# Attention, expert tiles and last norms of a Mamba and mixture-of-experts layer in one block, with rows routed in two parts

## The reference

```python
x = layernorm(x + mamba2(x) + x)
# one feed-forward layer:
qkv = x @ w_qkv                     # 16 heads of 8, causal attention in each row
o = attention(q, k, v) @ w_o
h = layernorm(x + o, g1, b1)
probs = softmax(h @ wg)             # 8 experts, top 2, weights made to sum to 1
h1 = gelu(h @ w1[e] + bb1[e])       # 128 -> 512, tanh form
y = h1 @ w2[e] + bb2[e]             # 512 -> 128
f = layernorm(h + sum of w * y, g2, b2)
x = layernorm(x + f)
```

## Time and profile before

| | |
|---|---|
| three runs | 1036.42, 1039.88 (median), 1048.26 us |
| the profiled execution | 1042.99 us, of which the span of the trace is 1041.2 us |
| TensorE busy | 749.1 us (72%) |
| VectorE busy | 649.8 us (62%) |
| ScalarE busy | 504.0 us (48%) |
| GpSimd busy | 393.9 us (38%) |
| DMA | 72.34 MB, 69 GB/s over the span |

### The profile page before, as it was taken

The page is one execution under the profiler, slowest core; times in us unless marked ns, Lnnn a source line. Parts: engine busy times, 40 slices in busy tenths (PEclk is TensorE's granted clock), DMA queues, the critical chain, the costliest instruction groups (busy, mean ns, idle before and its releaser), DMA issues. The chain is left out here.

```text
span 1041.2 us, 18849 instructions
## 1 busy us (share of the span) xinstructions
PE 749.1 (72%) x5297; PEld 505.1 (49%) x5298; DVE 649.8 (62%) x1639; ACT 504.0 (48%) x987; POOL 393.9 (38%) x500
## 2 busy tenths in 40 slices
PE   5788887887482669989898988888710999997000
PEld 3565666555352334535353544443310999997000
DVE  3888888896265747858586869772150454554585
ACT  3566555542171036545455555565400666675144
POOL 1233332233210012353535354644543355554254
PEclk8989988888595569989899999996855899999555
DMA  1000000000185312342424242312011222220241
GB/s 43 16 21 26 26 6 25 26 16 11 58 280 159 116 49 65 94 110 71 113 75 117 71 115 82 87 49 68 21 41 53 73 84 81 73 83 29 83 121 41
DMA packets 87082, 72.34 MB, mean 69 GB/s; under 512 B 10931, under 2 KB 78138, under 8 KB 87006
## 3 DMA queue, kind: packets, MB, share of 16 engines
q1 hardware_dynamic: 81726, 60.29, 20.7%
q0 software_dynamic: 5280, 11.13, 3.3%
HBM read 44.05 MB, written 22.12 MB: 64 GB/s over the span
## 5 line engine op out<-in xcount | busy, mean ns | idle before, releaser
L1350 ACT ACTIVATE pb<-psB 128x512 f32<-128x512 f32 (+1 forms) x352 | 186.2, 558 | 187.5 <-PE psB L1629 182.7
L1414 DVE TENSOR_REDUCE mx<-psB 128x1 f32<-128x384 f32 (+3 forms) x352 | 208.2, 633 | 92.8 <-PE psB L1611 92.5
L1609 PE MATMUL psB<-kx,qx 72*128 72x384 bf16 (+3 forms) x512 | 145.7, 336 | 19.2 <-DMA kx<-k_parts 19.1
L1629 PE MATMUL psB<-qx,kx 75*128 75x256 bf16 (+3 forms) x512 | 132.4, 320 | 29.5 <-DMA qx<-mparts 24.2
L1310 POOL TENSOR_SCALAR_AFFINE_SELECT pb<-pb 128x512 f32<-128x512 f32 x128 | 81.1, 639 | 162.7 <-ACT pb L1350 162.0
L1644 PE MATMUL psB<-pb,vx 128*32 128x512 f32 (+3 forms) x1024 | 104.3, 481 | 13.7 <-POOL pb L1310 13.7
L1611 PE MATMUL psB<-hide,ident 128*128 128x128 bf16 x512 | 109.7, 239 | 0.0
L1880 POOL DMA_INDIRECT results<-y_e,dest x72 | 70.0, 972 | 78.8 <-DVE y_e L1947 71.9
L1629 PEld LDWEIGHTS psB<-qx,kx 75*128 75x128 bf16 x512 | 44.9, 102 | 110.0 <-ACT pb L1350 52.7
L1940 DVE TENSOR_TENSOR pre<-psE,biases 128x512 f32<-128x512 f32 x72 | 49.8, 691 | 56.2 <-PE psE L1978 49.9
L1986 PE MATMUL psE<-w2s,gT 128*128 x576 | 80.0, 282 | 4.3 <-ACT gT L1909 4.3
(11 more groups left out here) (246 smaller groups left out, 1334.1 us busy)
## 6 DMA issues: line engine op xcount, KB each, us to landing
qx<-q_parts SPq DMA_DIRECT2D x96, 96.0 KB
kx<-k_parts SPq DMA_DIRECT2D x96, 96.0 KB
hin<-slots SPq DMA_DIRECT2D x72, 64.5 KB
ys<-results SPq DMA_DIRECT2D x16, 256.0 KB, 3.1
q_parts<-qpart SPq DMA_DIRECT2D x8, 384.0 KB
k_parts<-kpart SPq DMA_DIRECT2D x8, 384.0 KB
xin<-in_L_attn_X SPq DMA_DIRECT2D x8, 256.0 KB
x_rows<-x1o SPq DMA_DIRECT2D x8, 256.0 KB
```

Source lines behind the costliest of these rows:

```text
L1350: nc.scalar.activation(pb[step % PBUF][:, h0:h0 + heads, 0:width], src, ACT.Exp).then_inc(exp_ready, 2 if u == NEXP - 1 else 1)
L1414: nc.vector.tensor_reduce(mx[:, h0:h0 + heads, qt], ps[:, S_BANK + u % banks, 0:heads * width].rearrange("p (h n) -> p h n", n=width), AX. ...
L1609: nc.tensor.matmul(out, qx[q][0:QK_ROWS, h0 + j, qt * P:(qt + 1) * P], kx[q][0:QK_ROWS, h0 + j, 0:width], start=True, stop=False)
L1629: ins = nc.tensor.matmul(ps[:, E_BANK + u % E_BANKS, j * width:(j + 1) * width], kx[q][0:MAX_ROWS, 4 * g + h0 + j, kt * P:(kt + 1) * P], q ...
```

## The change

`attention_layer`, `experts` and `last_norms` become one function with one block and no barrier in it. Rows 0 to 4 and rows 5 to 7 are routed apart: each part has regions of its own in `slots`, its own counts, plan (26 steps) and fills. Part 0 needs at most 2 x 4 x 5 + 7 = 47 tiles, part 1 at most 31, together 78 (`JOBS`) in place of 72. The plan of part 0 and its fills stand in row 6's list.

Tiles go in "beats". In beat n TensorE does down(n), up(n+2), turn(n+3); ScalarE the turned copy of n+2, gelu(n+1) and `gate_result(n-1)`, which multiplies the result by the token's gate; VectorE the bias add of n+1 and the result of n; GpSimd stores tile n-2; SyncE loads tile n+7 and the w1 of tile n+5. Beats -3 to 6 stand in row 7's list, at slots 4, 8, ... 40. Behind row 7 comes a new list, `after()`, with beats 7 and up, and beside them what ends row 7, the routing of row 7, plan and fills of part 1, and the last norms: of rows 0 to 4 one each four beats from beat 52 on, of rows 5 to 7 in beats 83 to 85, behind the last tile.

w1 is no longer kept: each tile's w1 (256 KB) is loaded from DRAM into one of four buffers, at an offset of its own. The copy of w1 on ScalarE goes, as does the cast of the destination on VectorE: the payload carries it as an integer and also the gate. w2 loads in rows 1 and 2, all biases in row 3 (those of the first layer in pieces of 4 bytes). x1 is loaded again for each row's last norm. The last norms' two weighted sums (eight 128x128 operations per row) become two 128x512 additions. The tile buffers lie over the first row pair's q and k, the norms' over the second's.

The diff, cut to its core:

```diff
+SPLIT = 5
+PART_ROWS = (SPLIT, BATCH - SPLIT)
+PART_TILES = [TOPK * TILES * rows + E - 1 for rows in PART_ROWS]
+FIRST_TILE = [0, PART_TILES[0]]
+JOBS = sum(PART_TILES)
+RING = 12
...
+PLAN_ROW = SPLIT + 1
+PLAN_AT = [4 + i // 2 for i in range(PLAN)]
+FILL_AT = [8 + 3 * e for e in range(E)]
+FIRST_BEAT = -3
+EARLY_BEATS = {4 + 4 * i: FIRST_BEAT + i for i in range(10)}
+AFTER_BEAT = FIRST_BEAT + len(EARLY_BEATS)
+EARLY_TILES = AFTER_BEAT + 3
+TAIL = {"last heads": 1, "last out": 2, "last norm": 3, "last normalise": 5, "last gain": 5, "turn h": 8, "logits": 9,
+        "gate": 15, "ranks": 15}
+TAIL_CHAIN = [10 + i // 3 for i in range(14)] + [16 + i // 3 for i in range(CHAIN - 14)]
+TAIL_SCATTER = [19 + i for i in range(TOPK * TILES)]
+TAIL_PLAN = [19 + i // 3 for i in range(PLAN)]
+TAIL_FILL = [27 + e // 2 for e in range(E)]
+NORM_AT = [FIRST_TILE[1] + 5 + 4 * b for b in range(SPLIT)] + [JOBS + 5 + i for i in range(BATCH - SPLIT)]
+NORM_STEPS = {"sum": 0, "rstd 1": 0, "shift 1": 1, "norm 1": 1, "gain 2": 2, "residual": 3, "rstd 2": 3, "shift 2": 4, "norm 2": 4,
+              "store": 6}
...
+            def load_tile(j):
+                for g in range(2):
+                    if j == FIRST_TILE[g]:
+                        sp.wait_ge(planned[g], PLAN)
...
+                        sp.wait_ge(filled[g], 16 * E)
+                        sp.wait_ge(dead_filled, 32)
+                at = offset(sp, 0, j, SLOTS - P)
+                wait(sp, stored[j % RING], j // RING * 16)
+                sp.dma_start(hin[j % RING][:, :], slots[bass.ds(at, P), :]).then_inc(h_loaded[j % RING], 16)
+
+            def load_w1(j):
+                at = offset(sp, 3, j, (E - 1) * P)
+                wait(sp, up_ps, j - 3)
+                sp.dma_start(w1t[j % 4][:, :], w1.rearrange("e d f -> (e d) f")[bass.ds(at, P), :]).then_inc(w1_loaded[j % 4], 16)
...
+            def load_norm(b):
+                q = b % 2
+                if b in (0, SPLIT):
+                    tiles = FIRST_TILE[1] if b == 0 else JOBS
+                    for k in range(RING):
+                        sp.wait_ge(stored[k], 16 * ((tiles - k + RING - 1) // RING))
...
+                wait(sp, sum_ready, b - 1)
+                for k in range(TOPK):
+                    sp.dma_start(ys[q][:, k, :, :], results.rearrange("(k b t p) d -> k b p t d", k=TOPK, b=BATCH, p=P)[k, b]).then_inc(moe_in[q], 16)
+                wait(sp, lr_ready, b - 1)
+                sp.dma_start(x1r[q][:, :, :], x1_rows[b]).then_inc(x1_in[q], 16)
...
+            def store_result(j):
+
+                wait_apart(pool, gated, j + 1, pool_passed)
...
+            def turned(j):
+                act.wait_ge(ehT_ps, j + 1)
+                wait(act, up_ps, j - 1)
+                nc.scalar.activation(hTe[j % 2][:, :], ps[:, ht_bank(j), 0:P], ACT.Copy).then_inc(ehT_sb, 1)
+
+            def gelu(j):
+                act.wait_ge(pre_ready, j + 1)
+                wait(act, y_ps, j - 1)
+                nc.scalar.activation(gT[j % 2][:, :, :], pre[j % 2][:, :, :], ACT.Gelu_apprx_tanh).then_inc(g_ready, 1)
+
+            def gate_result(j):
+                act.wait_ge(y_ready, j + 1)
+                nc.scalar.activation(y[j % RING][:, :], y[j % RING][:, :], ACT.Copy, scale=hin[j % RING][:, D + 1:D + 2]).then_inc(gated, 1)
...
+                    elif what == "beat":
+                        if 0 <= n + 2 < JOBS:
+                            turned(n + 2)
+                        if 0 <= n + 1 < JOBS:
+                            gelu(n + 1)
+                        if 0 <= n - 1 < JOBS:
+                            gate_result(n - 1)
...
+            def moe_sum(b):
+                q = b % 2
+                dve.wait_ge(moe_in[q], (b // 2 + 1) * (16 * TOPK))
+                nc.vector.tensor_tensor(s0[q][:, :, :], ys[q][:, 0, :, :], ys[q][:, 1, :, :], ALU.add).then_inc(half_sum, 1)
+                dve.wait_ge(half_sum, b + 1)
+                wait(dve, n1_ready, b - 1)
+                nc.vector.tensor_tensor(s1[q][:, :, :], s0[q][:, :, :], h_all[:, b * TILES:(b + 1) * TILES, :], ALU.add).then_inc(sum_ready, 1)
...
+                    if what == "beat":
+                        if 0 <= n < JOBS:
+                            down(n)
+                        if 0 <= n + 2 < JOBS:
+                            up(n + 2)
+                        if 0 <= n + 3 < JOBS:
+                            turn(n + 3)
```

910 lines of the change are left out of this document (378 added, 532 removed).

## The result

The changed kernel takes 1061.16 us (median of 4 runs, 1059.63 to 1072.07), the kernel before beside it 1038.15 us (4 runs, 1026.85 to 1048.26). The ratio is 1.028, with a 95% interval of 1.016 to 1.040: slower, by more than the 1 per cent that the forecast took for no change. The forecast was 1013 us, with a range to 1046.

What follows compares the result with a forecast made beforehand. The prediction took a sum of stages, each with its own limit, to bound the kernel. 778 to row 7's last exponentials + 201 beats + 35 end = 1014 span, giving a 1013 us median; eight in ten between 980 and 1046.

Steps and rivals of the forecast that it cites:

- What bounds the kernel, the serial stages: Whole kernel: the end is set by a sum of stages, with 147 us of serial stages that the change overlaps.
- Rows 0 to 6 ... Sum +7; bounds 0 and +15: Attention rows before row 7: plan 4 us, masks delayed by fills 1, w2 and bias loads 2; together 7 us longer.
- Row 7, 70 us: Last attention row: 44 us plus 26 for eight gelu beats with table loads on ScalarE; exponentials end at 778.
- Beats, 201 us: Beats 7 to 77, behind row 7: 81 + 3 + 34 + 83 us, with SyncE at 2.4 us per beat, VectorE beside the norms.
- tiles 1.9 apart: Sign that the forecast is wrong: tiles come every 1.9 us, so SyncE's work is hidden.
- The first 31 beats: Row 7's last steps, routing, scatter and fills of part 1: 31 x 2.4 + 7 = 81 us, +3 for tile 47's wait.
- The next 14: Beats between the first 31 and the norms: 14 x 2.4 = 34 us at SyncE's pace.
- Beside the norms: Last 26 beats, five norms: VectorE decides, 13.7 us per norm and 4 beats, 83 us in all.
- The end, 35 us: Behind the last tile: path to the last loads, three norms at VectorE's pace 21 us, 3.2 to the end; 35 in all.
- TensorE's clock falls, and it is slower: Rival, chance 0.12: waiting in longer beats lowers TensorE's clock to 1.2 GHz, a beat's 1.89 us becomes 3.8; total over 1050.
- the weight loads bound: Rival, 0.18 together with row 7 serialising: slow w1 landings with four buffers set the beat, +25 us, 1038.
- idle time absorbs: Rival, chance two in ten: idle engine time takes the added work in rows, norms and routing; 38 us less, 975.

## Why the forecast was wrong, step by step

*What bounds the kernel, the serial stages:* right; three of the four stretches are gone.

*"Rows 0 to 6 ... Sum +7; bounds 0 and +15":* this step failed: row 7 starts 38 us later than in before. Three terms of it, and a fourth under them: the sum has no clock, though the granted clock over rows 1 to 6 fell to 0.73 to 0.90.
- The scatter's wait was not in the sum at all. The diff shows it (all 21 steps in place of 18, because the gates now travel in the payload), and the forecast's own method asks for it: what is queued behind a wait that the change adds. GpSimd's masks are. Put alone into the kernel before it made rows 1 to 6 29 us longer in the profile (6 rows by 2 us, and the clock), and taken out of the changed kernel it gave back 16 and 5.
- The biases were priced, together with the w2 loads, at 2 us. SyncE issues the eight loads of 4-byte pieces for 8.30 us, and row 4 pays for it, by 6 us at most in the runs with this edit alone and by 6 to 11 beside later scatters.
- The plan and fills were priced at 5, and row 6 grew by 12, a part of which is the scatter's wait: 3 go with the steps spread out. With the later scatters as well the row still takes 55 to 59 us, so for most of the 12 the cause stays open; VectorE has 42.86 us of work in 57.4. The forecast also read row 6 from a stretch of 39.7 us that begins inside it: the row lasts 45.3.

*Row 7, 70 us:* right, 67.3, with the 16 table loads forecast. The loads were all counted on the path, and some 12 of 20.5 us are, so the 4 us of idle time taken back were too few. The gated result takes 0.39 us a beat and not the 0.26 of a copy, 1 us in all. The row came out near 70 all the same; that TensorE's clock (0.86) took the difference is argued, not shown. The load takes 1283 ns and the next instruction follows at once, so the 1380 ns of drain that the Trainium skill, "ScalarE: Activation LUTs", What ACT_TABLE_LOAD costs, adds have no place here either: ScalarE sat idle 0.2 us in all before the 16 loads, and of 1.7 us before the 8 gelus 1.6 were waits for VectorE.

*Beats, 201 us:* the sum was right, 198.8, and the mechanism was not. The forecast made SyncE, at 2.4 us a beat, the bound of the first 45. SyncE takes 2.18, and with one offset read less on it nothing changes. Where tiles stand alone they come every 1.9 to 2.0 us at TensorE's pace, which is the forecast's own sign of being wrong ("tiles 1.9 apart"). The first 31 beats took 77.6 us against 84, and 77.7 with the lighter SyncE. The next 14 took 33.5 against 34 by luck: the wait for the fills, forecast at 3 in the piece before, fell among them with some 5. Beside the norms 3.2 was forecast from VectorE's sum and 3.3 measured. There too the sum was not the mechanism: VectorE is busy 43 of 76 us, and with the same work in smaller steps the pitch is 2.86. The lump, and the clock that is at half behind TensorE's waits, make the difference. A jump of 8.7 us at the first norm, in which VectorE stands 3.82 us in front of the first results, had no term.

*The end, 35 us:* failed, 52. The path from the last product to the first sum was right (8.6 us against 10). The three norms take 33 us and not 21: VectorE's 128x4 shift, 0.16 us otherwise, takes 1.22 to 1.25 in four of the last six cases, each time with a 128x512 operation of GpSimd beside it (its line in ns, min/median/max; before it was never over 164),

```profile
L1903 DVE SCALAR_TENSOR_TENSOR shift_l<-mv_l,rs_l x16: 152/164/1251, 930.1 to 1047.3; 128x4 f32<-128x4 f32 x16
```

```profile
L1110 POOLq DRAIN  x1: 10152/10152/10152, 1046.2 to 1046.2; - x1
...
L1110 SPq DRAIN  x1: 13/13/13, 1051.7 to 1051.7; - x1
L1110 SPq EVENT_SEMAPHORE  x1: 17/17/17, 1056.5 to 1056.5; - x1
```

and of the kernel before, its last block, its expert block and its qkv block:

```profile
L2009 POOLq DRAIN  x1: 1150/1150/1150, 1035.0 to 1035.0; - x1
```

```profile
L1794 POOLq DRAIN  x1: 5943/5943/5943, 961.3 to 961.3; - x1
```

```profile
L845 POOLq DRAIN  x1: 5433/5433/5433, 296.5 to 296.5; - x1
```

Before, GpSimd issued no transfer in the last block, and its drain cost nothing. The row was there to be read, in the 14.8 us of the stage boundary of the earlier trace rows.

*The rivals:* "TensorE's clock falls, and it is slower" is what happened, with a chance of 0.12, but mostly at another place: not in the middle beats (1.00), but in rows 1 to 6 and beside the norms (0.80), behind waits of TensorE, of some 2 us in the rows, not through a beat's length. That the weight loads bound is refuted: w1 landed in 2.6 us (median of 78). That idle time absorbs is refuted too.

*What stays open:* how much of the clock's movement belongs to a given edit, and why the same wait is followed by 6.8 us of half clock in one row and by 20.5 in another. Rows 1 to 6 take 323 to 340 us in nine profiles in which no edit touches them. And the changed kernel's total with later scatters alone, on a chip with a middle pitch of 2.3.

## What to carry to other kernels

When a change makes a queue wait for a little more, look up what stands behind the waiting instruction on that engine and whether TensorE needs it: 1.7 us a row made six rows of before 29 us longer in the profile. Work laid beside a pipeline of depth two has to be cut into pieces shorter than the pipeline's beat; its sum alone says little. And when serial stages are merged, price the joints (the wait, the issue of small-piece loads, the drain at the block's end) as carefully as the large terms, because the large ones were the easy part here.
